# Even and odd heads of an attention layer put into the lower and the upper 64 rows of TensorE's array

## The chip, the cores and the metric

The kernel runs on one core of one Trainium2 chip. The metric is the device time of one execution in microseconds, the median of several. The profiled execution is one more, and every duration below comes from it. PE is TensorE (its weight loads are listed as PEld), DVE VectorE, ACT ScalarE, POOL GpSimdE, SP SyncE, which here only issues DMAs.

## What is computed

The input x holds 64 images of 12 channels and 224 x 224 pixels.

```python
h = einsum("bcij,ce->bije", sums of 16x16 patches, channel_weights)   # 64 x 196 tokens x 192
h = h + single_head_attention(layernorm(h), Wq, bq, Wk, bk, Wv, bv)
h = h + experts(layernorm(h))     # 4 nested experts, each takes its best 98 of the 196 tokens
# inside experts, per image:
q, k, v = qkv.reshape(B, N, 3, 12, 16)...          # 12 heads of 16 columns
attn = softmax(einsum("bhqd,bhkd->bhqk", q, k) * 16 ** -0.5)
x_attn = einsum("bhqk,bhkd->bhqd", attn, v)        # beside gelu(x_mlp), then the second layer (w2)
```

## The kernel before, in words

**Tiling.** Images go in groups of eight (GRP), eight groups in all. A prologue pools and routes the first group; then a loop body runs the attention and the second layer of one group while the next one is pooled (DVE, `pool`), normed and routed (`choose` picks the best tokens). The last group has no next one. Before each group's body stands an opening of eight slots with the hidden layer of its images and the peaks of its first image.

**Order of work.** `body` and `opening` (lines 243 to 347) write out one list of operations: one slot per head, 12 per image, and every engine walks the same list and does its share of each operation. In slot h of image i stand `peak` of image i+1, head h; `score` of image i, head h; then the fill (second layer `fc2` of image i-1, `shift`, `norm_turn`, `project`, `values`, `residual`) and, in slots 1, 5 and 9, the `mix` of four heads. SP walks the list too: the write of the projection (line 709), the stacks (722), the shift row (730) and the output (737).

**Precision by parts.** Query and key are split into a high and a low f16 part (ACT casts at 1192, DVE subtracts at 1445) and written to a scratch in DRAM (709). `stack` reads them back with six DMAs per image into `qs` and `ks`: 16 rows each of (high, high, low) against (high, low, high), so that one matmul over these rows adds the three products. The stacks hold 97 rows: 48 with data, 48 that a memset has zeroed once (1489, 1565), and row 96 for the shift (all ones in `ks`, line 1567).

**Peaks and scores.** For each head PE does two matmuls over 96 rows (`peak`, line 986) into one of two peak banks, head h into bank h % 2, and DVE reduces the bank to the negated maximum of each query (1456). After six heads PE turns the peaks (995), ACT casts them into `shiftT` and one SP DMA puts them into row 96 of `qs` (730). Then two matmuls over 97 rows (`score`, 1005) give the transposed scores less their maximum in one of two score banks, ACT takes the exponential into `Pb` (1205), and `mix` (1020) multiplies with the values: eight matmuls of 32 columns, four heads side by side in four column strips of the array. A matmul in f32 appears in the trace as two.

**Waits.** `peak` waits for its own bank (`peak_free[s]`, counted by DVE), at h = 0 also for the image's stack; `score` waits for its own bank (`score_free[s]`, by ACT), at h = 0 and 6 also for the shift row.

Of the kernel before, what the change touches and what calls it, by code (L numbers as in the profile page):

```python
# [35 lines left out]
T = GRID * GRID  # L36
# [21 lines left out]
KS = 96  # L58
# [350 lines left out]
def bass_vit_tower(nc, x, cw, Wq, bq, Wk, bk, Wv, bv, w_router, gamma, beta, w1, b1, w2, b2, consts, out):  # L409
# [9 lines left out]
    with ctx:  # L419
# [50 lines left out]
        qk16 = sb("qk16", [DC, 2, 2, 2, T], F16)  # L470
        qs = sb("qs", [KS + 1, NSTACK, H, T], F16)
        ks = sb("ks", [KS + 1, NSTACK, H, T], F16)
# [73 lines left out]
        gp_in = sem("gp_in")  # L546
# [123 lines left out]
        def _(sp):  # L670
# [33 lines left out]
            def project(at, G_, dg, i):  # L704

                n_ = G_ * GRP + i
                sp.wait_ge(hi_ready, 2 * n_ + 2)
                sp.wait_ge(lo_ready, 2 * n_ + 2)
                sp.dma_start(qk_dram[i % 2].rearrange("m s c d (h t) -> (d h) (m s c) t", t=T),
                             qk16[:, :, :, :, :].rearrange("p m s c t -> p (m s c) t")).then_inc(qk_out, 16)  # L710

            def stack(at, G_, dg, i):
# [33 lines left out]
        def _(pe):  # L746
# [232 lines left out]
            def peak(at, G_, dg, i, h):  # L979

                s = h % 2
                if h == 0:
                    pe.wait_ge(stack_in[i % NSTACK], 96 * (len(range(i % NSTACK, GRP, NSTACK)) * G_ + i // NSTACK + 1))
# [14 lines left out]
            def score(at, G_, dg, i, h):  # L998

                s = h % 2  # L1000
                if h % 6 == 0:
                    pe.wait_ge(shift_in[h // 6], 16 * (GRP * G_ + i + 1) + ONE)
                pe.wait_ge(score_free[s], 6 * (GRP * G_ + i) + h // 2 + ONE)
                for k in range(2):
                    mm = pe.matmul(score_ps[s][0:HT, T * k:T * k + T],  # L1005
                                   ks[:, i % NSTACK, h, HT * k:HT * k + HT], qs[:, i % NSTACK, h, :],
                                   start=True, stop=True)
                mm.then_inc(score_full[s], 1)
# [57 lines left out]
        def _(act):  # L1066
# [15 lines left out]
            def fuse(at, G_, dg, part):  # L1082
# [8 lines left out]
                for n4, (f, end) in enumerate(M_PARTS):  # L1091
                    dst, src = M[:, f:end], banks[n4][0:U, 0:end - f]
                    if f == HID:
                        dst = dst.rearrange("u (n d h) -> u n h d", d=DH, h=H // 2)
                        src = src.rearrange("u (n h d) -> u n h d", d=DH, h=H // 2)
# [90 lines left out]
            def project(at, G_, dg, i):  # L1186
                n_ = GRP * G_ + i
                act.wait_ge(qk_out, 16 * n_ + ONE)
                for m in range(2):
                    slot, k = at.uses(("qk"[m], (dg, i)))  # L1190
                    act.wait_ge(misc_full[slot], k + 1)
                    act.copy(qk16[:, m, 0, :, :].rearrange("p c t -> p (c t)"), misc_ps[slot][0:DC, 0:2 * T]) \  # L1192
                        .then_inc(hi_ready, 1)

            def shift(at, G_, dg, i, part):
                n_ = GRP * G_ + i
                ps, free = ring(at, "shift", (dg, i, part))
                act.wait_ge(shift_in[part], 16 * n_ + ONE)
                evac(shiftT[:, part, :], ps[0:6, 0:T], free, shift_ready, 2 * n_ + part + 1)

            def score(at, G_, dg, i, h):
                s = h % 2
                n_ = GRP * G_ + i
                act.wait_ge(score_full[s], 6 * n_ + h // 2 + 1)
                act.activation(Pb[:, (H * i + h) % NP, :, :].rearrange("p a b -> p (a b)"), score_ps[s][0:HT, 0:2 * T],  # L1205
# [436 lines left out]
```

## Time and profile before

| | us |
|---|---|
| median of 3 runs | 1775.73 (1774.58 to 1777.63) |
| profiled execution | 1772.98 |
| its span, first to last instruction | 1771.2 |
| PE busy | 1519.9 (86%) |
| DVE busy | 1218.1 (69%) |
| ACT busy | 848.6 (48%) |
| mean granted TensorE clock | 0.921 of full |

Busy time is the union of an engine's instructions over the span. Matmuls overlap, so their mean length is more than the distance between two starts, and the ends of matmuls are modelled. The chain that ended last follows the work back from the last instruction, at each step to what released it. The first 205 us are setup and the prologue; after that a group takes about 201 us, and the last one 155.

### The profile page before, as it was taken

To read this page: it belongs to the slowest core of one execution; us is meant where nothing else is said; L and a number is where in the kernel's file an instruction comes from. 1 tells how busy PE (TensorE), PEld (TensorE's weight loads), DVE (VectorE), ACT (ScalarE), POOL (GpSimd) and SP (SyncE) were. 2 spreads that over 40 slices of the span, in tenths; PEclk is the share of its full clock that TensorE was granted. 3 is DMA by queue.
4 is the path that set the end of the run, shared out by engine and by line. 5 is a ranking of instruction groups with operands and counts; after the bars stand their busy time and mean duration, and the time that the engine had idled before them with its cause. 6 is when DMAs were issued, how large, how long until landed. Compare 5 with 4: busy or idle time off the path is not lost.

```text
span 1771.2 us, 34644 instructions
## 1 busy us (share of the span) xinstructions
PE 1519.9 (86%) x12440; PEld 1260.6 (71%) x12440; DVE 1218.1 (69%) x2822; ACT 848.6 (48%) x1935; POOL 249.4 (14%) x318
## 2 busy tenths in 40 slices
PE   1364689998998899989998899999899889989998
PEld 1233567777786777778787777778677778878786
DVE  3847678766887578865887568875787567563552
ACT  0101355545554555545654554545554555546654
POOL 2012002200121002200121002210022002110000
PEclk9757689989999999999999989989998899989999
DMA  9867376706573357606664356615656151102220
GB/s 225 233 166 195 89 179 158 188 15 161 148 187 99 85 148 178 184 16 158 156 168 117 76 145 168 180 40 136 165 149 148 35 145 45 42 19 59 50 53 15
DMA packets 99598, 218.03 MB, mean 123 GB/s; under 512 B 61371, under 2 KB 75877, under 8 KB 88678
## 3 DMA queue, kind: packets, MB, share of 16 engines
q10 hardware_dynamic: 11904, 149.33, 31.3%
q1 hardware_dynamic: 87526, 66.49, 16.5%
q8 instruction: 102, 1.67, 0.4%
q14 instruction: 66, 0.54, 0.1%
HBM read 186.57 MB, written 28.90 MB: 122 GB/s over the span
## 4 chain that ended last, share of the span: by engine, by line
PE 50%; DVE 25%; issue 13%; DMA 5%; POOL 3%; ACT 2%; SPq 1%; DVEq 0%; ACTq 0%; POOLq 0%
PE bank L1051 13%; DVE psums L1256 10%; DVE peaks L1456 6%; PE bank L956 6%; PE bank L986 5%; PE bank L1020 5%; PE bank L1005 4%; DMA qs<-shiftT 3%; POOL var L1585 3%; PE bank L968 2%; PE bank L879 2%; PE bank L830 2%; PE bank L1029 2%; PE bank L943 2%; DVE qk L1445 1%
## 5 line engine op out<-in xcount | busy, mean ns | idle before, releaser
L1456 DVE TENSOR_REDUCE peaks<-bank 98x2 f32<-98x392 f32 x768 | 423.6, 563 | 170.3 <-PE bank L986 149.3
L1205 ACT ACTIVATE Pb<-bank 98x392 f32<-98x392 f32 x768 | 374.9, 497 | 300.1 <-PE bank L1005 250.9
L1256 DVE TENSOR_REDUCE psums<-xt 112x2 f32<-112x512 f32 x672 | 425.7, 677 | 27.1 <-DVE peaks L1456 9.7
L1051 PE MATMUL bank<-w2T,hid 128*98 128x192 f32 x1536 | 311.4, 342 | 0.0
L986 PE MATMUL bank<-ks,qs 96*98 96x196 f16 x1536 | 268.4, 261 | 42.8 <-DVE peaks L1456 37.9
L1005 PE MATMUL bank<-qs,ks 97*98 97x196 f16 x1536 | 268.3, 258 | 22.1 <-DMA qs<-shiftT 20.2
L986 PEld LDWEIGHTS bank<-ks,qs 96*98 96x98 f16 x1536 | 165.5, 128 | 132.7 <-DVE peaks L1456 66.2
L1051 PEld LDWEIGHTS bank<-w2T,hid 128*98 128x98 f32 x1536 | 249.5, 176 | 3.5
L1005 PEld LDWEIGHTS bank<-qs,ks 97*98 97x98 f16 x1536 | 167.3, 130 | 34.5 <-DMA qs<-shiftT 22.9
L1020 PE MATMUL bank<-Pb,vals 98*32 98x196 f32 x3072 | 171.9, 342 | 1.2 <-ACT Pb L1205 1.2
L1613 POOL TENSOR_TENSOR fin<-fin,both 98x384 f32<-98x384 f32 x64 | 63.9, 999 | 732.9 <-DVE fin L1481 732.9
L956 PE MATMUL bank<-UT,M 104*128 104x196 f32 x768 | 150.8, 347 | 16.9 <-DVEq L1450 16.9
L956 PEld LDWEIGHTS bank<-UT,M 104*128 104x128 f32 x768 | 133.7, 200 | 21.8 <-DVEq L1450 19.3
L1183 ACT ACTIVATE hid<-bank 128x392 f32<-128x392 f32 x192 | 93.5, 497 | 109.9 <-PE bank L956 109.7
L1445 DVE TENSOR_TENSOR qk<-bank,qk 96x392 f16<-96x392 f32 x128 | 71.7, 560 | 84.6 <-ACT qk L1192 74.6
L1576 POOL TENSOR_TENSOR spread_p<-psums,cst 112x196 f32<-112x196 f32 x96 | 50.0, 521 | 533.2 <-DVE psums L1256 533.2
L1020 PEld LDWEIGHTS bank<-Pb,vals 98*32 98x32 f32 x3072 | 81.3, 110 | 54.2 <-issue 25.0
L1117 ACT COPY oT<-bank 128x196 f32<-128x196 f32 x192 | 61.9, 322 | 106.8 <-PE bank L1020 102.4
L1051 PE MATMUL bank<-w2T,onT 96*98 96x192 f32 (+1 forms) x512 | 108.3, 334 | 0.0
L968 PE MATMUL bank<-UT,M 104*96 104x196 f32 x512 | 99.0, 337 | 0.1
L830 PE MATMUL bank<-spread_p,cst 112*24 112x196 f32 x192 | 44.4, 376 | 48.8 <-POOL spread_p L1576 43.3
L1585 POOL TENSOR_TENSOR var<-var,cst 98x16 f32<-98x16 f32 x24 | 69.7, 2904 | 106.7 <-DVE var L1289 58.7
(183 smaller groups left out, 1783.6 us busy)
## 6 DMA issues: line engine op xcount, KB each, us to landing
xt<-in_x_dram ACTq DMA_DIRECT2D x93, 1568.0 KB, 9.0
qk_scratch<-qk SPq DMA_DIRECT2D x64, 294.0 KB, 4.1
qs<-qk_scratch SPq DMA_DIRECT2D x192, 73.5 KB, 3.0
ks<-qk_scratch SPq DMA_DIRECT2D x192, 73.5 KB, 3.1
out_dram<-fin SPq DMA_DIRECT2D x64, 147.0 KB
xt<-in_x_dram SPq DMA_DIRECT2D x3, 1568.0 KB, 8.8
qs<-shiftT SPq DMA_DIRECT2D x128, 2.3 KB
hid<-in_L_ffn_w_dram SPq DMA_DIRECT2D x1, 1440.0 KB
```

The source lines that it names most:

```text
L956: mm = pe.matmul(ps[:, T * j:T * j + T], M[:, 128 * f:128 * f + 128], UT[:, i, :], start=True, stop=True)
L968: mm = pe.matmul(ps[0:DC, T * c:T * c + T], M[:, f:f + DC], UT[:, i, :], start=True, stop=True)
L986: mm = pe.matmul(peak_ps[s][0:HT, T * q:T * q + T], qs[0:KS, i % NSTACK, h, HT * q:HT * q + HT], ks[0:KS, i % NSTACK, h, :], start=True, s ...
L1005: mm = pe.matmul(score_ps[s][0:HT, T * k:T * k + T], ks[:, i % NSTACK, h, HT * k:HT * k + HT], qs[:, i % NSTACK, h, :], start=True, stop=True)
L1020: mm = pe.matmul(ps[32 * j:32 * j + 32, 0:T], vals[:, i % 2, q, h, :], Pb[:, (H * i + h) % NP, q, :], start=(q == 0), stop=(q == 1))
L1051: mm = pe.matmul(misc_ps[slot][0:HT, D * h:D * h + D], lhs, w2T[0:w, f, :], start=(f == 0), stop=(f == NF + 1))
L1183: act.activation(hid[:, i, 2 * b:2 * b + 2, :].rearrange("p a b -> p (a b)"), ps[:, 0:2 * T], ACT.Gelu).then_inc(free, 1)
L1205: act.activation(Pb[:, (H * i + h) % NP, :, :].rearrange("p a b -> p (a b)"), score_ps[s][0:HT, 0:2 * T], ACT.Exp, scale=float(DH) ** -0.5 ...
L1256: last = dve.tensor_reduce(psums[:, m % 2, t, 2 * p:2 * p + 2], v[:, 2 * p:2 * p + 2, :, :], AX.XY, ALU.add)
L1445: dve.tensor_tensor(qk16[:, m, 1, :, :].rearrange("p c t -> p (c t)"), misc_ps[slot][0:DC, 0:2 * T], qk16[:, m, 0, :, :].rearrange("p c t ...
L1456: dve.tensor_reduce(peaks[:, h // 6, :, h % 6], peak_ps[s][0:HT, 0:2 * T].rearrange("p (q k) -> p q k", q=2), AX.X, ALU.max, negate=True). ...
L1585: gp.tensor_tensor(var[:, 2, :], var[:, 1, :], const("half", HT), ALU.pow).then_inc(gp_pow, 1)
```

## The change

Even heads lie in rows 0 to 63 of the stacks and odd heads in rows 64 to 127, each with 48 rows of data and the shift in the 49th. The zero rows go. Peaks and scores are issued for two heads at a time, in even slots: first columns of the even and of the odd head, then the second columns of both. Each half has its own bank. Both banks are waited for ahead of the first matmul. The fill of the slots keeps its order. The columns of the projection are laid out anew (when M is copied, with one ACT copy more), so that heads of one parity lie together; ACT and DVE write the high and low parts to other places of `qk16`. The stack of an image is read with eight DMAs in place of six (the same bytes), and each shift part with two in place of one. The memset of `qs` goes and those of `ks` become smaller.

```diff
-KS = 96
+KS = 3 * DH
+ODD = 64
...
-        qs = sb("qs", [KS + 1, NSTACK, H, T], F16)
-        ks = sb("ks", [KS + 1, NSTACK, H, T], F16)
+        qs = sb("qs", [2 * ODD, NSTACK, H // 2, T], F16)
+        ks = sb("ks", [2 * ODD, NSTACK, H // 2, T], F16)
...
             def stack(at, G_, dg, i):
...
-                for blk, (qp, kp) in enumerate(((0, 0), (0, 1), (1, 0))):
-                    for m, st, part in ((0, qs, qp), (1, ks, kp)):
-                        sp.dma_start(st[DH * blk:DH * blk + DH, s, :, :].rearrange("d (c h) t -> d c (h t)", c=2),
-                                     qk_dram[i % 2, m, part].rearrange("c d w -> d c w")) \
+                for m, st in enumerate((qs, ks)):
+                    for c in range(2):
+                        both_ = qk_dram[i % 2, c, m].rearrange("s d w -> (s d) w")
+                        low = ODD * c
+                        sp.dma_start(st[low:low + 2 * DH, s, :, :].rearrange("d h t -> d (h t)"), both_) \
                             .then_inc(stack_in[s], 16)
+                        sp.dma_start(st[low + 2 * DH:low + KS, s, :, :].rearrange("d h t -> d (h t)"),
+                                     both_[DH * (1 - m):DH * (1 - m) + DH, :]).then_inc(stack_in[s], 16)
...
-                sp.dma_start(qs[KS:KS + 1, i % NSTACK, 6 * part:6 * part + 6, :],
-                             shiftT[:, part, :]).then_inc(shift_in[part], 16)
+                for c in range(2):
+                    sp.dma_start(qs[ODD * c + KS:ODD * c + KS + 1, i % NSTACK, 3 * part:3 * part + 3, :],
+                                 shiftT[3 * c:3 * c + 3, part, :]).then_inc(shift_in[part], 16)
...
             def peak(at, G_, dg, i, h):
-                s = h % 2
+                if h % 2:
+                    return
...
-                pe.wait_ge(peak_free[s], 6 * (GRP * G_ + i) + h // 2 + ONE)
+                for s in range(2):
+                    pe.wait_ge(peak_free[s], 6 * (GRP * G_ + i) + h // 2 + ONE)
                 for q in range(2):
-                    mm = pe.matmul(peak_ps[s][0:HT, T * q:T * q + T],
-                                   qs[0:KS, i % NSTACK, h, HT * q:HT * q + HT], ks[0:KS, i % NSTACK, h, :],
-                                   start=True, stop=True)
-                mm.then_inc(peak_full[s], 1)
+                    for s in range(2):
+                        mm = pe.matmul(peak_ps[s][0:HT, T * q:T * q + T],
+                                       qs[ODD * s:ODD * s + KS, i % NSTACK, h // 2, HT * q:HT * q + HT],
+                                       ks[ODD * s:ODD * s + KS, i % NSTACK, h // 2, :], start=True, stop=True)
+                        if q == 1:
+                            mm.then_inc(peak_full[s], 1)
...
             def score(at, G_, dg, i, h):
...
+                for s in range(2):
+                    pe.wait_ge(score_free[s], 6 * (GRP * G_ + i) + h // 2 + ONE)
                 for k in range(2):
+                    for s in range(2):
+                        mm = pe.matmul(score_ps[s][0:HT, T * k:T * k + T],
+                                       ks[ODD * s:ODD * s + KS + 1, i % NSTACK, h // 2, HT * k:HT * k + HT],
+                                       qs[ODD * s:ODD * s + KS + 1, i % NSTACK, h // 2, :], start=True, stop=True)
+                        if k == 1:
+                            mm.then_inc(score_full[s], 1)
...
-            dve.memset(qs[:, :, :, :], 0.0)
...
-            gp.memset(ks[:, :, :, :], 0.0).then_inc(gp_in, 1)
-            gp.wait_ge(gp_in, 1)
-            gp.memset(ks[KS:KS + 1, :, :, :], 1.0).then_inc(zeroed, 1)
+            gp.memset(ks[ODD // 2:ODD, :, :, :], 1.0)
+            gp.memset(ks[ODD + ODD // 2:2 * ODD, :, :, :], 1.0).then_inc(zeroed, 1)
```

DVE's `peak` and ACT's `score` change likewise: in even slots they reduce, or exponentiate, first the even and then the odd head. The peaks of the even heads of a part come first in `peaks`, then those of the odd heads.

## Rows read from the trace of the kernel before

**Rows 1.** The page: span, busy time and share of two engines, the chain by engine.
```profile
span 1771.2 us, 34644 instructions
...
PE 1519.9 (86%) x12440; PEld 1260.6 (71%) x12440; DVE 1218.1 (69%) x2822; ACT 848.6 (48%) x1935; POOL 249.4 (14%) x318
...
PE 50%; DVE 25%; issue 13%; DMA 5%; POOL 3%; ACT 2%; SPq 1%; DVEq 0%; ACTq 0%; POOLq 0%
```

**Rows 2.** Busy time by stretch: from:to, us, each engine, then clock, DMA share, GB/s.
```profile
674.00:704.00 30.00, 28.89 (x253) 24.30 (x251) 26.29 (x56) 14.28 (x34) 8.33 (x12) 1.00 0.57 142
704.00:730.00 26.00, 25.86 (x231) 21.77 (x230) 20.73 (x45) 16.29 (x38) 5.41 (x11) 1.00 0.71 183
...
1600.00:1760.00 160.00, 150.77 (x1376) 128.81 (x1375) 76.26 (x167) 94.36 (x212) 8.43 (x9) 0.99 0.19 45
```

The engines in this view stand in the order PE, PEld, DVE, ACT, POOL.

**Rows 3.** The chain in order of time, 640 to 842 us: start, length, what.
```profile
654.20 6.28 DMA qs<-shiftT
...
751.75 1.92 PE bank L1051 x6
...
775.83 0.98 PE bank L1051 x6
```

**Rows 4.** Groups of instructions: busy us, mean ns | idle before, and who ended it.
```profile
L1456 DVE TENSOR_REDUCE peaks<-bank 98x2 f32<-98x392 f32 x768 | 423.6, 563 | 170.3 <-PE bank L986 149.3 <-DVE on_tok L1469 1.1 <-DVE qk L1445 0.8
...
L986 PE MATMUL bank<-ks,qs 96*98 96x196 f16 x1536 | 268.4, 261 | 42.8 <-DVE peaks L1456 37.9 <-DMA ks<-qk_scratch 0.2
L1005 PE MATMUL bank<-qs,ks 97*98 97x196 f16 x1536 | 268.3, 258 | 22.1 <-DMA qs<-shiftT 20.2 <-ACT Pb L1205 1.6
```

**Rows 5.** Timeline of PE from 778.4 us; one row of its weight loads last.
```profile
778.48 0.81 PE L1051 MATMUL bank<-w2T,onT 96*98 96x192 f32 x4
779.22 0.87 PE L1020 MATMUL bank<-Pb,vals 98*32 98x196 f32 x16
780.02 0.37 PE L986 MATMUL bank<-ks,qs 96*98 96x196 f16 x2
780.23 0.33 PE L1005 MATMUL bank<-qs,ks 97*98 97x196 f16 x2
780.40 0.33 PE L986 MATMUL bank<-ks,qs 96*98 96x196 f16 x2
780.57 0.33 PE L1005 MATMUL bank<-qs,ks 97*98 97x196 f16 x2
...
780.32 0.21 PEld L986 LDWEIGHTS bank<-ks,qs 96*98 96x98 f16 x2
```

**Rows 6.** Timeline of PE in the setup, transposes of line 814.
```profile
59.80 0.26 PE L814 MATMUL bank<-cst,hid 64*96 64x64 f32 x1
59.99 0.31 PE L814 MATMUL bank<-cst,hid 128*96 128x128 f32 x1
60.14 0.93 PE L814 MATMUL bank<-cst,hid 128*96 128x128 f32 x7
```

**Rows 7.** Who waited for whom: us in total, times, longest us.
```profile
PE bank L986 <- DVE peaks L1456: 37.9, 65, 1.4
...
PE bank L1005 <- DMA qs<-shiftT: 20.2, 13, 3.6
```

**Rows 8.** SP's queue: its longest wait, and its issues (ns min/median/max).
```profile
SPq L730 <- ACT shiftT L1117: 680.6, 128, 11.6
...
L730 SPq DMA_DIRECT2D qs<-shiftT x128: 664/685/741, 223.0 to 1746.0; - x128
...
L722 SPq DMA_DIRECT2D ks<-qk_scratch x192: 414/424/2179, 202.3 to 1720.5; - x192
```

**Rows 9.** Busy time around a stretch at half clock (columns as in rows 2).
```profile
745.60:749.00 3.40, 1.32 (x9) 0.78 (x10) 2.07 (x9) 0.71 (x4) 1.93 (x2) 1.00 1.04 270
749.00:755.80 6.80, 6.80 (x31) 5.90 (x30) 4.65 (x13) 1.67 (x4) 2.90 (x1) 0.50 0.78 169
```

More of the change, by code:

```diff
@@ L998, in score @@
             def score(at, G_, dg, i, h):
-                s = h % 2
+                if h % 2:
+                    return
                 if h % 6 == 0:
-                    pe.wait_ge(shift_in[h // 6], 16 * (GRP * G_ + i + 1) + ONE)
-                pe.wait_ge(score_free[s], 6 * (GRP * G_ + i) + h // 2 + ONE)
+                    pe.wait_ge(shift_in[h // 6], 32 * (GRP * G_ + i + 1) + ONE)
+                for s in range(2):
+                    pe.wait_ge(score_free[s], 6 * (GRP * G_ + i) + h // 2 + ONE)
                 for k in range(2):
[L1005 to L1008, printed above, removed]
+                    for s in range(2):
[4 more added lines that the diff above has]
+                            mm.then_inc(score_full[s], 1)
             def mix(at, G_, dg, i, c):
@@ L1093, in fuse @@
                     if f == HID:
-                        dst = dst.rearrange("u (n d h) -> u n h d", d=DH, h=H // 2)
-                        src = src.rearrange("u (n h d) -> u n h d", d=DH, h=H // 2)
+                        dst = dst.rearrange("u (m c d h) -> u m c d h", m=2, c=2, d=DH)
+                        src = src.rearrange("u (m h c d) -> u m c d h", m=2, c=2, d=DH)
+                        act.copy(dst[:, 0], src[:, 0])
+                        dst, src = dst[:, 1], src[:, 1]
                     last = act.copy(dst, src)
@@ L1191, in project @@
                     act.wait_ge(misc_full[slot], k + 1)
-                    act.copy(qk16[:, m, 0, :, :].rearrange("p c t -> p (c t)"), misc_ps[slot][0:DC, 0:2 * T]) \
+                    act.copy(qk16[:, :, 1 + m, :], misc_ps[slot][0:DC, 0:2 * T].rearrange("p (c t) -> p c t", c=2)) \
                         .then_inc(hi_ready, 1)
@@ L1197, in shift @@
                 ps, free = ring(at, "shift", (dg, i, part))
-                act.wait_ge(shift_in[part], 16 * n_ + ONE)
+                act.wait_ge(shift_in[part], 32 * n_ + ONE)
                 evac(shiftT[:, part, :], ps[0:6, 0:T], free, shift_ready, 2 * n_ + part + 1)
             def score(at, G_, dg, i, h):
-                s = h % 2
+                if h % 2:
+                    return
                 n_ = GRP * G_ + i
-                act.wait_ge(score_full[s], 6 * n_ + h // 2 + 1)
-                act.activation(Pb[:, (H * i + h) % NP, :, :].rearrange("p a b -> p (a b)"), score_ps[s][0:HT, 0:2 * T],
-                               ACT.Exp, scale=float(DH) ** -0.5).then_inc(score_free[s], 1)
+                for s in range(2):
+                    act.wait_ge(score_full[s], 6 * n_ + h // 2 + 1)
+                    act.activation(Pb[:, (H * i + h + s) % NP, :, :].rearrange("p a b -> p (a b)"),
+                                   score_ps[s][0:HT, 0:2 * T],
+                                   ACT.Exp, scale=float(DH) ** -0.5).then_inc(score_free[s], 1)
             def mix(at, G_, dg, i, c):
@@ L1444, in project @@
                     dve.wait_ge(hi_ready, n_)
-                    dve.tensor_tensor(qk16[:, m, 1, :, :].rearrange("p c t -> p (c t)"),
-                                      misc_ps[slot][0:DC, 0:2 * T],
-                                      qk16[:, m, 0, :, :].rearrange("p c t -> p (c t)"),
+                    dve.tensor_tensor(qk16[:, :, 3 * m, :],
+                                      misc_ps[slot][0:DC, 0:2 * T].rearrange("p (c t) -> p c t", c=2),
+                                      qk16[:, :, 1 + m, :],
                                       ALU.subtract).then_inc(lo_ready, 1)
@@ L1452, in peak @@
             def peak(at, G_, dg, i, h):
-                s = h % 2
+                if h % 2:
+                    return
                 n_ = 6 * (GRP * G_ + i) + h // 2 + 1
-                dve.wait_ge(peak_full[s], n_)
-                dve.tensor_reduce(peaks[:, h // 6, :, h % 6],
-                                  peak_ps[s][0:HT, 0:2 * T].rearrange("p (q k) -> p q k", q=2),
-                                  AX.X, ALU.max, negate=True).then_inc(peak_free[s], 1)
-                if h % 6 == 5:
-                    dve.wait_ge(peak_free[s], n_ + ONE)
+                for s in range(2):
+                    dve.wait_ge(peak_full[s], n_)
+                    dve.tensor_reduce(peaks[:, h // 6, :, h % 6 // 2 + 3 * s],
+                                      peak_ps[s][0:HT, 0:2 * T].rearrange("p (q k) -> p q k", q=2),
+                                      AX.X, ALU.max, negate=True).then_inc(peak_free[s], 1)
+                if h % 6 == 4:
+                    for s in range(2):
+                        dve.wait_ge(peak_free[s], n_ + ONE)
                     dve.sem_inc(peaks_ready, 1)
```

9 lines of the change are left out of this document (4 added, 5 removed).

## The prediction

> **What bounds the kernel now.** I read the page first [rows 1]: PE is busy for 86% of the span, DVE for 69%, and the chain that ended last is half PE and a quarter DVE. An average over stages says little, so I then read one group of eight images, from 640 to 842 us, by stages and beside it the chain in order of time [rows 2, 3]. The reader is to see that the stages differ. From 674 to 704 us DVE is busy for 26.3 of 30 us and the chain hops from one DVE instruction to the next (sums of the next group, peaks, first-layer maxima). From 704 to 730, 747 to 760 and 770 to 813 us it runs over PE (fc2, hidden, mixes). Adding up the chain's PE stretches (641 to 644, 660 to 674, 704 to 730, 747 to 760, 770 to 813, 817 to 828 and 834 to 838 us) gives 113 of the 202 us. One matmul cut out of PE is therefore worth its price in a little over half of a full group. In the last group no new images are pooled, DVE is busy for 76 of 160 us, PE for 151, and PE's time counts almost in full (last line of [rows 2]).
>
> **What a head costs now.** Peaks and scores are 1536 matmuls each [rows 4], two per head. Their means (261 and 258 ns) are lengths from issue to result; what they cost is the distance from one start to the next. In a stretch without waits the starts lie at 780.23, 780.40 and 780.57 us, so one head of peaks or of scores costs 0.17 us [rows 5]. Their weight load costs nothing there, because it starts one matmul ahead: at 780.32 for the matmul of 780.40.
>
> **The array's halves.** With 48 or 49 rows at row 0 and at row 64 an even and an odd head can stream together. No row of this trace shows two row halves at once; the bounds are 0.17 us for two heads (full overlap) and 0.34 (none). The nearest row is the mix: 16 matmuls into four column strips take 0.80 us from 779.22 to 780.02, four waves at 0.165 with four matmuls in each and one change of form [rows 5], while one f32 matmul of fc2 costs 0.163 alone (0.98 for six) [rows 3]. Four strips at once cost what one does, so I take full overlap, 0.175 us for two heads. That saves 0.165 us per pair. A full group has 48 pairs of peaks and 48 of scores: 96 x 0.165 = 15.8 us.
>
> **What it pays for that.** The trace charges for each change between forms of the array. From fc2 (four matmuls, 0.65) at 778.48 to the mix at 779.22 are 0.74 us, 0.09 more; after a mix the same 0.09 comes again, and the next weight load lies bare: the head at 780.02 is 0.21 long, not 0.17 [rows 5]. Forms cut by rows pay too: a 64-row transpose in the setup starts at 59.80 us and its 128-row neighbour at 59.99, 0.19 later, though it streams half as many columns as the 128-row ones, which lie 0.11 apart (seven of them from 60.14, 0.93 to the end of the last, 0.27 long) [rows 6]. The Trainium skill says the same against this change ("TensorEngine Tiling (Array Packing)", Key Properties): changing the tiling mode, not just the tile, drains TensorE. It gives no price; by the rows it is 0.09. I counted the changes of form along PE's order, written out by the planner. Peaks and scores of a pair mostly stand together and are followed by full-height work or a mix. A full group goes from 66 changes to 141: 75 x 0.09 = 6.8 us. Loads laid bare: 32 entries from full-height work at 0.04 = 1.3; 47 exits, of which 31 into f32 matmuls, whose 98 to 128 columns of weights have about 0.08 to lose, and 16 into transposes or the like at 0.04: 3.1. Net for PE in a full group: -15.8 + 6.8 + 1.3 + 3.1 = -4.6 us. Added up operation by operation, half of it falls into the PE stretches named above, because the pairs alone in the opening (peaks without scores, +0.13 each) stand there too: -2.3. Seven such groups: -16.1. The last group: 90 pairs save 14.9, 58 more changes cost 5.2, bare loads 3.3: -6.4. The prologue's six lone pairs: +0.8. **Sum on PE: -21.7 us.**
>
> **Waits.** A pair now waits for both peak banks and both score banks. Behind that wait on PE's queue stand the scores, fc2 and everything else; DVE and ACT wait for these. Today PE waits 37.9 us, 65 times, for DVE's peaks [rows 7]. At worst each of those waits grows by the odd head's reduction, 0.563 us [rows 4]: +36. At best they vanish, -38: DVE now gets both reductions ahead of the other work of two slots, ahead of the projection's two subtractions above all. DVE waits for PE's peaks four times as long (149.3 us [rows 4]) as PE for it, and after both reductions it has 1 to 2 us of other work before it needs the next pair, against the 0.2 us of PE's reply. I take 0. ACT is busy for little more than half of any stretch in [rows 2]: 0.
>
> **SyncE's queue.** The shift row is sent by two DMAs in place of one, 128 more issues at 0.685 us [rows 8]. They are behind a wait for ACT's shiftT, and both must land before the first score of a half. PE waits for this DMA 13 times, 20.2 us in all [rows 7]. If the second issue delays each: 13 x 0.685 = +8.9; if the landing is set by what else the DMA engines move (one chain piece has 6.28 us from issue to use, nine times the issue [rows 3]), 0. I take half, +4.5. The stacks are eight DMAs per image where there were six, the same bytes: 128 more issues at 0.42 = 54 us of SyncE's time. The queue waits 680.6 us for shiftT alone [rows 8], and a stack is due one image later: 0. If that cover went, PE's wait for the stack (0.2 us today, under ks<-qk_scratch in [rows 4]) would grow first. The projection's write keeps its size.
>
> **Clock.** In this group PE runs at half its rate (1.2 in place of 2.4 GHz) four times. In the 3.4 us ahead of the first of them it had been busy for 1.32 us, and then for all of 6.8 us at half rate [rows 9]. At half rate six matmuls of fc2 take 1.92 in place of 0.98 us [rows 3]. The halves make PE stream less, and in stretches where DVE or a DMA sets the pace nothing fills the hole. Bounds: no further stretch, 0; one of 6.8 us in each of eight groups, half of it lost, +27. I take one of 3.4 us in every second full group, 1.7 lost in each, and as much again in longer ones: +6.
>
> **Setup.** The memset of qs goes and those of ks shrink; they run before the first tile of x is there, which DVE waits for. The copy of M gets one instruction more, once: 0. Subtractions and casts of q and k keep their shapes: 0.
>
> **Sum.** -21.7 + 4.5 + 6 = -11.2. The profiled execution took 1773.0 us (its span 1771.2 [rows 1]), 2.7 under the median of 1775.7. 1773.0 - 11.2 = 1761.8, and with those 2.7 the median forecast is **1764.5 us**.
>
> **Rivals.**
> First, **no overlap** (the change doesn't do what it says): the two halves stream one after the other. Then the 0.165 are not saved and the changes of form are paid: +11.2 us on PE per full group, half of it in the chain, 7 x 5.6, last group +8.5, prologue +1.8, with shift and clock +10.5: 1836 us. For it: no row shows two row halves together. Against: the column strips, in the same rows as above. It decides if over 0.29 us of the 0.34 remain. 10%.
> Second, **partial overlap**: both halves' weights come one after the other, and each wave lays one load bare, 0.04. 192 waves: +7.7 us, so +3.1 per full group, 7 x 1.55, last group +0.8, prologue +1.3, others +10.5: 1799 us. For it: a bare load shows as 0.04 at each entry. Against: the mix, where four matmuls and their four loads fit into one wave. 12%.
> Beside this stands the Trainium skill ("TensorE: Matmul & The Clock Gate", Measured speedup vs the span model): four row strips ran 3.07 times as fast, 0.77 of full; no run here shows it. By that figure a pair would cost 0.22 us and the time would be about 1785, an estimate from that page.
> Third, **the clock**, the case that ends on the other side: PE drops to half rate in one 6.8 us stretch more per group, +27 in place of +6: 1785 us; it decides from about 2 us lost per group. For it: the stretches where PE waits for a shift or for POOL are at the edge already. Against: where PE sets the pace it is busy throughout, 25.9 of 26 us [rows 2]. 12%.
> Fourth, **both banks as one** on DVE's side: the +36 above, 1800 us. For it: the DVE stretch from 674 to 704 us. Against: the order of work on DVE. 8%.
>
> **Chances and range.** My forecast 53%, with its own range 1738 (two thirds of the peak waits vanish, -26) to 1772 (the whole 8.9 for the shift row, and 3 more for the clock). The four rivals 42%; the rest is a change too small to see. About 0.2%, 3.6 us, is what a measurement can tell from no change. Faster 0.53; same 0.12, from the forecast's upper end and the weak forms of the third and fourth case; slower 0.35. The range 1738 to 1801 leaves out the first rival and the tails.
>
> **What the new profile would show.** Right: in a stretch without waits, even and odd head start within some 10 ns, the next pair's start lies 0.17 to 0.18 us behind; PE's matmuls of peaks and scores have about half the busy time of today's 268 us each; idle put down to "issue" before them grows by 51 x 0.25 us or so per group; the reductions of DVE come in twos. Wrong: starts of the halves 0.08 us apart (first rival), pairs at 0.21 or more (second), more than five half-rate stretches per group (third), PE's wait for DVE's peaks above 60 us (fourth), PE's wait for the shift row above 30 us.

## The result, and the profile after

The changed kernel took 1812.6 us (median of 4 runs, 1810.3 to 1815.5) against 1776.7 for the kernel before (1774.6 to 1781.0): a ratio of 1.020, interval 1.018 to 1.023. That is 36 us slower, where 11 us faster had been forecast, and above the upper end of the range (1801). Ratios leave out executions more than 1.5% above the fastest of the same kernel, so they need not be the quotient of the medians.

The page of the kernel after: span, busy time of the engines, granted clock in 40 slices, and the chain by engine, as in [rows 1].

```profile
span 1813.7 us, 35428 instructions
...
PE 1521.1 (84%) x12440; PEld 1167.1 (64%) x12440; DVE 1208.7 (67%) x2821; ACT 809.4 (45%) x1936; POOL 242.7 (13%) x318
...
PEclk9757789888997879979798879979888899989898
...
PE 49%; DVE 24%; issue 12%; DMA 6%; POOL 3%; SPq 3%; ACT 2%; DVEq 0%; POOLq 0%; ACTq 0%
```

PE is busy for 1521 us, as long as before (1520), though its two f16 groups have lost nearly half their time: other work of PE has become longer (L1063 below was 311.4 us before). The next views show where. First the groups of instructions, as in [rows 4]: busy us, mean ns | idle before.

```profile
L1063 PE MATMUL bank<-w2T,hid 128*98 128x192 f32 x1536 | 323.1, 356 | 0.0
L993 PE MATMUL bank<-ks,qs 48*98 48x196 f16 x1536 | 154.4, 281 | 80.9 <-DVE peaks L1475 71.9 <-DMA ks<-qk_scratch 8.5
...
L1016 PE MATMUL bank<-qs,ks 49*98 49x196 f16 x1536 | 148.0, 272 | 20.5 <-DMA qs<-shiftT 14.5 <-ACT Pb L1221 5.9
```

Peaks and scores (L993, L1016) went from 268 us each to 154 and 148. The idle time before the peaks grew from 42.8 to 80.9 us. Then the timeline of PE in a stretch at full clock.

```profile
702.46 0.37 PE L993 MATMUL bank<-ks,qs 48*98 48x196 f16 x4 [0.36 <-DVE peaks L1475]
702.64 0.36 PE L1016 MATMUL bank<-qs,ks 49*98 49x196 f16 x4
702.94 0.33 PE L1003 MATMUL bank<-cst,peaks 98*6 98x98 f32 x2
```

Four matmuls, a pair of heads, take 0.18 us from start to start, where one head took 0.17 [rows 5]: the halves do stream together. After the scores the exit from the 64-row form (the array split into two halves of rows) shows: 0.30 us to the next operation instead of 0.17 or 0.18. Ahead of the pair of peaks PE has waited 0.36 us for DVE. Now who waited for whom (us in total, times, longest).

```profile
PEld bank L993 <- issue: 92.0, 273, 2.2
...
PE bank L993 <- DVE peaks L1475: 71.9, 74, 2.1
...
PE bank L1016 <- DMA qs<-shiftT: 14.5, 11, 2.0
```

The wait for DVE's peaks nearly doubled (37.9 in [rows 7]), the one for the shift row fell (20.2), and the weight loads of peaks sat idle under "issue" for 92.0 us, 50.4 before. Last, the stretches at half clock (1.2 in place of 2.4 GHz); columns as in [rows 2], the clock third from the end.

```profile
762.30:776.00 13.70, 11.62 (x58) 8.09 (x58) 8.48 (x27) 3.32 (x10) 6.29 (x3) 0.50 0.57 154
...
864.70:885.20 20.50, 19.61 (x132) 12.79 (x131) 15.06 (x30) 10.48 (x26) 0.52 (x1) 0.50 0.39 96
```

Before, no half-clock stretch between 250 and 1350 us was longer than 6.8 us. Adding up the granted clock's record from 205 us on gives 347 us at half clock in 41 stretches, against 167 in 32 before. A group in the middle has five or six such stretches, 48 to 58 us together; before it had four or five, 20 to 24 us.

So four things stand in the profile: overlap (gain), changes of form, a longer wait for a bank, and more half-clock time. The experiments price the first three; the clock moves with each of them and isn't separated.

### The profile page after: what moved, and what is told of

Its sections match the earlier page's. It is cut to its first block, busy times and chain, and to the rows that moved or that the text cites. A ratio compares the mean times of both kernels' runs of the same rounds, so it can differ in the third digit from the quotient of the medians.

```text
span 1813.7 us, 35428 instructions
## 1 busy us (share of the span) xinstructions
PE 1521.1 (84%) x12440; PEld 1167.1 (64%) x12440; DVE 1208.7 (67%) x2821; ACT 809.4 (45%) x1936; POOL 242.7 (13%) x318
## 4 chain that ended last, share of the span: by engine, by line
PE 49%; DVE 24%; issue 12%; DMA 6%; POOL 3%; SPq 3%; ACT 2%; DVEq 0%; POOLq 0%; ACTq 0%
PE bank L1063 13%; DVE psums L1273 9%; DVE peaks L1475 7%; PE bank L960 6%; PE bank L1032 5%; PE bank L993 4%; PE bank L972 3%; DMA ks<-qk_scratch 3%; POOL var L1603 3%; PE bank L1016 3%; PE bank L883 2%; PE bank L1041 2%; PE bank L834 2%; PE bank L947 2%; DVE nm L1320 1%
## 5 line engine op out<-in xcount | busy, mean ns | idle before, releaser
L1475 DVE TENSOR_REDUCE peaks<-bank 98x2 f32<-98x392 f32 x768 | 398.1, 561 | 183.4 <-PE bank L993 171.0
L1221 ACT ACTIVATE Pb<-bank 98x392 f32<-98x392 f32 x768 | 339.3, 494 | 255.2 <-PE bank L1016 233.9
L1063 PE MATMUL bank<-w2T,hid 128*98 128x192 f32 x1536 | 323.1, 356 | 0.0
L1063 PEld LDWEIGHTS bank<-w2T,hid 128*98 128x98 f32 x1536 | 265.1, 182 | 16.9 <-issue 5.8
L993 PE MATMUL bank<-ks,qs 48*98 48x196 f16 x1536 | 154.4, 281 | 80.9 <-DVE peaks L1475 71.9
L993 PEld LDWEIGHTS bank<-ks,qs 48*98 48x98 f16 x1536 | 71.0, 128 | 189.6 <-issue 92.0
L1032 PE MATMUL bank<-Pb,vals 98*32 98x196 f32 x3072 | 186.0, 364 | 1.4 <-ACT Pb L1221 1.4
L1016 PE MATMUL bank<-qs,ks 49*98 49x196 f16 x1536 | 148.0, 272 | 20.5 <-DMA qs<-shiftT 14.5
L1462 DVE TENSOR_TENSOR qk<-bank,qk 96x392 f16<-96x392 f32 x128 | 71.9, 561 | 93.7 <-ACT qk L1206 82.9
L1016 PEld LDWEIGHTS bank<-qs,ks 49*98 49x98 f16 x1536 | 91.2, 137 | 35.4 <-DMA qs<-shiftT 17.0
L1063 PE MATMUL bank<-w2T,onT 96*98 96x192 f32 (+1 forms) x512 | 112.9, 344 | 0.0
L972 PEld LDWEIGHTS bank<-UT,M 104*96 104x96 f32 x512 | 83.4, 173 | 13.1 <-issue 3.8
```

What stands on the lines that cost most here:

```text
L972: mm = pe.matmul(ps[0:DC, T * c:T * c + T], M[:, f:f + DC], UT[:, i, :], start=True, stop=True)
L993: mm = pe.matmul(peak_ps[s][0:HT, T * q:T * q + T], qs[ODD * s:ODD * s + KS, i % NSTACK, h // 2, HT * q:HT * q + HT], ks[ODD * s:ODD * s + ...
L1016: mm = pe.matmul(score_ps[s][0:HT, T * k:T * k + T], ks[ODD * s:ODD * s + KS + 1, i % NSTACK, h // 2, HT * k:HT * k + HT], qs[ODD * s:ODD ...
L1032: mm = pe.matmul(ps[32 * j:32 * j + 32, 0:T], vals[:, i % 2, q, h, :], Pb[:, (H * i + h) % NP, q, :], start=(q == 0), stop=(q == 1))
L1063: mm = pe.matmul(misc_ps[slot][0:HT, D * h:D * h + D], lhs, w2T[0:w, f, :], start=(f == 0), stop=(f == NF + 1))
L1221: act.activation(Pb[:, (H * i + h + s) % NP, :, :].rearrange("p a b -> p (a b)"), score_ps[s][0:HT, 0:2 * T], ACT.Exp, scale=float(DH) ** ...
```

## The experiments

Beside each set of runs the kernel before ran on the same chip (medians of 1774.6 to 1777.4 us, from 12 to 19 runs); ratios are to it. Half-clock times and waits are those of one profiled execution.

**1. Pairs in full height** (e1): the kernel before with heads issued in pairs and both banks waited for, on the old 96-row stacks.

```diff
+                if h % 2:
+                    return
+                for s in range(2):
+                    pe.wait_ge(peak_free[s], 6 * (GRP * G_ + i) + h // 2 + ONE)
+                for s in range(2):
+                    for q in range(2):
...
```

> The kernel before with peaks, scores, reductions and exponentials in pairs and both banks waited for, but each head still over 96 or 97 rows: nothing overlaps, no form of the array changes, the DMAs stay. Theory 'clock' (the change loses its time because PE streams fewer columns and so runs longer at half clock): PE streams as much as before, so the half-clock time after 205 us stays within 30 us of before's 167 us and the time within 0.5% of 1776 (1768 to 1786). Theory 'both banks' (the joint wait is what costs): most of the 36 us of the change is here, 1800 to 1815, with PE's wait for DVE's peaks above 60 us.

1797.2 us, ratio 1.014 (1.010 to 1.018), clock 0.912. More than half of the loss comes without any half of the array. PE's wait for DVE's peaks was 69.7 us and half clock 200 us.

**2. Everything twice in the halves** (e2): the kernel after with each matmul of peaks and scores repeated (`for q in (0, 0, 1, 1)`).

> The changed kernel with each matmul of peaks and scores done twice, so that PE streams for them as long as before the change (0.35 us for a pair in place of 0.175), with all the changes of form besides: PE has some 16 us more to do per group. Theory 'clock': the half-clock time falls from 347 us towards 170 to 220, and the extra work costs little or nothing: 1795 to 1820 us, no slower than the change. Theory 'changes of form' or 'both banks' (the clock is a result, not the cause): the extra streaming comes on top, 8 to 16 us per group, 1875 to 1930 us.

1850.0 us (1.041; 1.037 to 1.045), 37 above the kernel after by the medians, for some 130 us more of streaming on PE, between the two expectations. Half clock was 174 us in place of 347, in the fastest of the four runs (granted clock 0.921, 0.910 in the others, 0.872 in the kernel after). So 127 us of streaming are worth 37 us here, under a third: a first hint that what the overlap saves is worth less than forecast.

**3. The DMAs alone** (e3): the kernel before with eight stack DMAs per image and two for each shift row.

```diff
+                for c in range(2):
+                    sp.dma_start(qs[KS:KS + 1, i % NSTACK, 6 * part + 3 * c:6 * part + 3 * c + 3, :],
+                                 shiftT[3 * c:3 * c + 3, part, :]).then_inc(shift_in[part], 16)
```

> The kernel before with the change's DMAs alone: eight for each stack and two for each part of the shift row. My sum had +4.5 us for this, bounds 0 and 9. Theory 'clock' and theory 'both banks': 1776 to 1786. Theory 'DMAs' (SP's longer queue delays the shift row and the stacks): at least half of the 36 us, 1795 or more, with PE's wait for the shift row above 35 us in place of 20.

1774.4 us, ratio 0.9985 (0.996 to 1.001); PE waits 15.2 us for the shift row, 13 times, and 4.2 us for the stack (0.2 before). The DMAs cost nothing that can be measured.

**4 and 5. PE kept busy** (e4 on the kernel after, e5 on the kernel before): extra f32 matmuls into banks about to be overwritten, at four places where PE is short of work.

```diff
+            def busy(bank, n):
+                for _ in range(n):
+                    pe.matmul(bank[:, 0:T], ident, cst[:, 0:T], start=True, stop=True)
...
+                busy(ps, 7)
```

> The changed kernel with useless f32 matmuls (0.165 us for each of the two parts of one) into the bank about to be written, ahead of PE's long waits: 3 at planes, 7 at chosen, 6 at the first hidden of a group, 2 at each pair of peaks of the second image. They add work but no result. Theory 'clock': half-clock time after 205 us falls from 347 us below 200 and the time falls by 10 to 45 us, to 1765 to 1800. Theories 'both banks' and 'changes of form': no gain, 1812 to 1830.

1813.7 us (1.0225; 1.020 to 1.025), half clock 160 us in place of 347, clock 0.931: the clock came back and the time stayed. The extra work took 122 us of PE's busy time, so this run alone doesn't say what the clock was worth.

> The kernel before with the same extra f32 matmuls as e4 (three at each image pair's planes, seven ahead of the choice, six ahead of the first hidden, one per peak of image 1), which raised the clock of the kernel after from 0.872 to 0.931 and left its time at 1813.7. Theory A (the extra matmuls themselves cost PE time, and in the kernel after the clock's return paid for them): the kernel before, whose clock was 0.921, has little to get back and pays, 1785 to 1800. Theory B (the extra matmuls lie in idle time and cost nothing, so the clock was worth nothing either): 1770 to 1780.

1810.7 us (1.020; 1.013 to 1.027), half clock 68 us. That is more than the 1785 to 1800 of the nearer expectation. The same extra work costs the kernel before 34 us and the kernel after 1. I read the difference as the clock: of the kernel after 187 us of half clock were taken away, of the kernel before 100, and the 87 us between them paid 32 us, 0.37 us each. This isn't shown: it supposes that the extra work alone costs both the same, and with the joint wait PE waits 83.5 us for DVE's peaks in e4 (58.3, and 25.2 ahead of the extra matmuls), 32.7 in e5.

**6. Pairs, each head with its own wait** (e6): e1, with the wait for a bank directly ahead of that head's matmuls.

```diff
                 for s in range(2):
                     pe.wait_ge(peak_free[s], 6 * (GRP * G_ + i) + h // 2 + ONE)
-                for s in range(2):
                     for q in range(2):
```

> e1 (the kernel before, full height, heads issued in pairs) came out at 1797.2 us. Here PE waits for a head's own bank just before that head's two matmuls instead of for both banks ahead of the pair; VectorE and ScalarE still take two heads in a row. Theory A, the joint wait costs the time (the pair starts only when the later of two banks is free): back to about 1778, within 5. Theory B, the order costs it (a pair of peak reductions or exponentials placed in one slot delays what stood between them): it stays at 1797, within 5.

1771.8 us, ratio 0.9987 (0.9955 to 1.002): no loss. The waits of PE's peaks in e1:

```profile
PE bank L989 <- DVE peaks L1467: 69.7, 80, 1.7
...
PE bank L989 <- DMA ks<-qk_scratch: 11.1, 7, 2.7
```

and in e6:

```profile
PE bank L988 <- DVE peaks L1465: 31.7, 44, 1.3
...
PE bank L988 <- DMA ks<-qk_scratch: 13.0, 7, 2.6
```

The order on VectorE and ScalarE is the same in both, and the late stack is alike (11 and 13 us), half clock nearly so (200 and 184 us). Of PE's waits the one for VectorE differs most, 38 us; the one for ScalarE's exponentials is 3.8 us in e1 and 0.8 in e6. The joint waits, for peak and score banks together, cost 25 us, nothing else in the pairs does. How they do is my reading: two banks become one, PE stands while DVE reduces the second head, then DVE stands while PE streams (DVE's wait for PE's peaks is 154.9 us in e1, 142.6 in e6).

**7 and 8. Only peaks, only scores in pairs** (e7, e8): the parts of e1.

> The kernel before with only the peaks in pairs (PE with both banks waited for, VectorE two reductions in a row); scores as before. Theory A, what VectorE gives back late is what PE waits for (in e1 the wait of the peak matmuls on VectorE's peaks was 69.7 us against 37.9): nearly all of e1's 21 us, 1790 to 1797. Theory B, it is the scores, whose pair puts two exponentials in front of ScalarE's other evacuations and shifts the project step and its stack transfer: under 5 us, 1775 to 1781.

> The kernel before with only the scores in pairs. Theory A of e7: 1775 to 1781. Theory B of e7: 1790 to 1797. If the two parts add, this run and e7 together lose e1's 21 us.

1795.7 and 1795.8 us (both 1.012; 1.007 to 1.017 and 1.006 to 1.018). Each part alone loses nearly all of what both lose. They don't add, and neither theory fitted. In e7 PE waits 63.9 us for VectorE's peaks. Why scores alone lose as much isn't settled, since PE's wait there for VectorE's peaks is 42.7 us and for ScalarE 10.1: the wait for the peaks isn't the whole of what a joint wait costs. Scores in pairs with own waits alone were not run.

**9. Halves, one head per slot** (e9): the kernel after with the old slots, own waits, no pairs.

> The kernel after with its 64-row halves and stacks, but one head per slot with its own bank's wait, as before: no two halves meet except where one head's last matmul stands beside the next head's first. Theory A, the pairing and its waits cost 21 us and the halves themselves cost only their change of form: PE streams as much as before plus up to 7 us of changes per group hidden in part, 1776 to 1795. Theory B, the halves are what costs (changes of form and clock): no better than the kernel after, 1808 to 1830, since the overlap is lost as well.

1968.1 us, ratio 1.110 (1.103 to 1.116), far outside both theories. From 205 us on PE enters or leaves the 64-row form 1402 times instead of 816. Half clock was 454 us, in an execution in which PE was busy for 89% of the span, more than in any other. The 27.3 us from 691 us on are one stretch at half clock, columns as above:

```profile
691.00:718.30 27.30, 26.53 (x144) 17.06 (x144) 17.22 (x34) 12.13 (x28) 0.52 (x1) 0.50 0.38 90
```

**10 and 11. Halves with own waits.** e10 waits for the odd bank after the first even matmul; e11 issues even 0, even 1, wait, odd 0, odd 1; its edit, made alike in `score`:

```diff
                 for s in range(2):
                     pe.wait_ge(peak_free[s], 6 * (GRP * G_ + i) + h // 2 + ONE)
-                for q in range(2):
-                    for s in range(2):
+                    for q in range(2):
```

> The kernel after, but PE waits for the second bank only after the first matmul of the even head: even 0, wait, odd 0, even 1, odd 1; still two heads at a time. In full height the pair with a joint wait cost 21 us (1797.2) and the pair with each head's own wait nothing (1771.8). Theory A, it is the joint wait in the kernel after too, and one matmul ahead of it is enough: 1790 to 1800. Theory B, the halves' interleaved order hands both banks over together at the end of the pair, so that VectorE and ScalarE still start late and the next pair still waits for the second of two reductions: 1806 to 1815, little better than the kernel after (1812.6).

> The kernel after in the order even 0, even 1, wait, odd 0, odd 1: each head's bank is handed over as early as in the full-height pairs with own waits, one entry and one exit of the 64-row form per pair as in the kernel after, but only one of the two halves streams at a time save where even 1 meets odd 0. Theory A (early hand-over is worth more than the overlap): 1785 to 1800. Theory B (the changes of form cost on their own: one head at a time they cost 193 us over 768 visits, 0.25 us each; in pairs there are half as many visits, some 96 us, no longer paid by the overlap of 0.165 us per two matmuls): 1830 to 1880.

1803.7 us (1.016; 1.008 to 1.024) and 1804.6 (1.017; 1.010 to 1.024). Both lie between their two expectations. All eight runs (1796 to 1808) lie below all four of the kernel after (1810 to 1816), though the intervals of the ratios overlap. The wait for VectorE's peaks fell to 44.4 and 40.2 us. e11 should have lost its overlap by my own reckoning, but it did not. Its timeline, with the odd bank free at 703.8 and late at 710.0:

```profile
703.81 0.37 PE L992 MATMUL bank<-ks,qs 48*98 48x196 f16 x4
704.02 0.34 PE L1014 MATMUL bank<-qs,ks 49*98 49x196 f16 x4
704.28 1.57 PE L972 MATMUL bank<-UT,M 104*96 104x196 f32 x8
...
710.05 0.70 PE L992 MATMUL bank<-ks,qs 48*98 48x196 f16 x3
710.47 0.28 PE L1014 MATMUL bank<-qs,ks 49*98 49x196 f16 x1
```

Four matmuls again pass in 0.21 us. The single records show even 0 at 703.812, odd 0 at 703.819, even 1 at 703.935, odd 1 at 703.941; which record is which follows from the semaphores recorded with them (the odd bank's wait stands at the second record, the even bank's increment at the third). So by the records the odd head overtook the even head's second matmul. That happened in 304 of 384 pairs of peaks and 301 of 384 of scores. Where the odd bank is late, both even matmuls go first. The Trainium skill ("TensorE: Matmul & The Clock Gate", The mechanism) has matmuls in strict order of issue; the records of e11 don't agree.

**12. Extra matmuls ahead of the choice alone** (e13): the kernel before plus the seven of e5 in each group, where PE waits for VectorE's choice.

> The kernel before with only the seven extra matmuls ahead of the choice. There PE stands idle while VectorE chooses; in e4 the stretch from the peaks of image 6 on was 3.5 us per group shorter than in the kernel after. Theory A (half clock in the opening of a group costs, and work in the idle stretch ahead of it returns it): 1745 to 1768. Theory B (VectorE sets the end of that stretch whatever the clock): 1772 to 1782.

1753.1 us (10 runs, 1746.0 to 1762.0), ratio 0.988 (0.985 to 0.991): the one version that beats both kernels. Half clock fell from 167 to 105 us. From the first reduction of one group to that of the next, four groups in the middle took 196.5, 199.8, 196.2 and 202.4 us, before 201.4, 201.2, 203.8 and 205.2.

**13 and 14. The same seven on pairs** (e14 on e6, e15 on e10).

> Full-height pairs with own waits (e6, 1771.8) plus the seven extra matmuls ahead of the choice, which took the kernel before from 1777.1 to 1753.1. If pairs with own waits are worth nothing and the filler's gain is its own, 1746 to 1756; if fewer visits of PE per head help once the clock is up, below 1745; if the two hinder each other (e6 had the image stack landing late seven times), 1757 to 1770.

> The halves with the second bank waited for after the first matmul (e10, 1803.7, half clock 327 us) plus the same seven extra matmuls. Theory A (the clock is what the halves lose): the filler returns more here than the 24 us of the kernel before, 1755 to 1772. Theory B (changes of form are what they lose): it returns 24 us or less, 1780 to 1795, and stays some 30 us behind e14.

1773.2 us (0.998; 0.994 to 1.002) and 1797.6 (1.014; 1.008 to 1.020). Both lie above their expectations, and the gain isn't carried over: half clock stays at 181 us in e14 (184 in e6) and at 304 in e15 (327 in e10). Why the order of the pairs keeps its half-clock stretches wasn't tried.

**15 to 17. Changes of form alone** (e16, again as e19 in more rounds) and their control (e17): e6 with one small matmul ahead of each pair of peaks, over 48 rows (64-row form) or over 96.

```diff
+                    if s == 0:
+                        pe.matmul(peak_ps[0][0:HT, 0:8], qs[0:48, i % NSTACK, h, 0:HT],
+                                  ks[0:48, i % NSTACK, h, 0:8], start=True, stop=True)
```

> Full-height pairs with own waits (e6) plus one matmul of 48 rows and 8 columns in the 64-row form ahead of each pair of peaks: PE enters and leaves the 64-row form 384 times more, and streams 3072 columns more in all, about 1.3 us. Theory A (changes of form cost what they show, 0.09 us and more each, part of it on the path): 25 to 60 us above e6, 1797 to 1832, and above e17. Theory B (they hide in PE's idle time, the halves lose by the clock): within 8 us of e17.

> The control for e16: the same small matmul with 96 rows, in the form of the pair itself. Both theories: within 8 us of e6, 1766 to 1780, since it only adds a weight load of 98 columns and 8 streamed columns per pair.

> The same kernel as e16, whose runs took 1790 to 1829 us. If its fast runs again stand 20 to 45 us above e17's 1778.0, the changes of form are shown; below 1785 they were not what e16 paid.

e16: 1819.4 us (four runs, 1790 to 1829; 1.017; 1.005 to 1.029). e19: 1822.8 (1811 to 1827), ratio 1.024 (1.021 to 1.027). e17: 1778.0, ratio 1.002 (0.999 to 1.005). The timeline of e19:

```profile
700.70 0.20 PE L988 MATMUL bank<-ks,qs 48*98 48x8 f16 x1
700.84 0.54 PE L991 MATMUL bank<-ks,qs 96*98 96x196 f16 x4
```

and of e17:

```profile
703.19 0.17 PE L988 MATMUL bank<-ks,qs 96*98 96x8 f16 x1
703.22 0.52 PE L991 MATMUL bank<-ks,qs 96*98 96x196 f16 x4
```

From the small matmul to the pair are 0.14 us with a change of form and 0.03 without (up to 0.07 elsewhere in e17), so that a change shows as 0.07 to 0.11 us, around the 0.09 of [rows 5]. The weight loads' idle time under "issue" goes the way of the kernel after, in e19:

```profile
PEld bank L988 <- issue: 82.5, 282, 1.1
PE bank L988 <- DVE peaks L1468: 20.0, 39, 1.3
```

against 42.4 us, 114 times, in e17. PE's busy time is 1607.8 us in e19 and 1542.1 in e17, 0.086 us more for each of the 768 changes. In time they cost 45 us by the medians (1822.8 - 1778.0) and 39 by the ratios, 51 to 58 ns each, nearly two thirds of the 0.09 us that one shows on PE. Half clock is 225 us, 194 in e17, so a part of this comes by way of the clock.

**18. Half the columns** (e18): e6 with 98 streamed columns in place of 196 in five pairs of six; about 105 us less to stream (3072 matmuls x 5/6 x 98 columns at 2.4 GHz). The kernel leaves out the other half of these products, and its exponential has a scale near zero, so only its time counts.

> Full-height pairs with own waits (e6, 1771.8) that stream 98 columns instead of 196 in the peaks and scores of five pairs of each six, about as much less as the overlap saves, with no 64-row form. It leaves out the other half of those products, and the exponential's scale is near zero. Theory A (the saved columns lie on PE's path, and the halves lose by changes of form): 1735 to 1755. Theory B (fewer columns lengthen the half-clock time, which takes them back): half clock well above e6's 184 us and a time of 1762 to 1780.

1766.4 us (9 runs, 1746.9 to 1780.4), ratio 0.991 (0.987 to 0.994). Against e6 that is 5 us by the medians, 14 by the ratios. Page and waits of e18's profiled execution (its fastest):

```profile
span 1745.1 us, 34596 instructions
...
PE 1459.2 (84%) x12440; PEld 1202.6 (69%) x12440; DVE 1207.7 (69%) x2822; ACT 804.7 (46%) x1935; POOL 248.7 (14%) x318
```

```profile
PE bank L988 <- DVE peaks L1467: 49.8, 111, 1.7
...
PE bank L1010 <- DMA qs<-shiftT: 17.1, 12, 4.9
```

Peaks and scores are busy for 335 us, in e6 for 435: 100 less. All of PE has only 65 less (1524.0 in e6), so by this account the other matmuls took 35 us more; half clock rose from 184 to 252 us. And PE waits longer for VectorE's peaks (49.8, in e6 31.7) and for the shift row (17.1 and 9.0). Theory A fell and theory B came, in its time and in its sign. By the forecast's price of 0.56 the 105 us were worth 59. An estimate accounts for most of what is missing: 68 us more of half clock at the 0.37 of e4 and e5 are 25 us, and PE's waits for peaks, shift row and stack are 23 us longer. So the saved columns seem to go into clock and waits; how much into which isn't shown.

## Why the prediction was wrong

The parts, put together from the runs and beside my terms:

| term | forecast | measured, from |
|---|---|---|
| pairs as such | 0 | -3, e6 to the kernel before beside it; not clear of zero |
| less streaming | -71 | -7 to -17, e18 scaled from 105 to 127 us; -37, e2 |
| changes of form, loads laid bare | +50 | +34 to +47, e19 to e17, scaled |
| joint wait | 0 | +6 to +8, kernel after to e11 (+25 in full height) |
| DMAs of the shift row | +4.5 | 0, e3 |
| clock, as a term | +6 | not separated; lies in the terms above |
| sum | -11 | +20 to +45 by e18, 0 to +15 by e2; the result was +36 |

The forecast's second and third entry are my -21.7 taken apart: 11.2 us of changes and loads per full group, half of them in the chain for seven groups, 8.5 in the last and 1.8 in the prologue make 50, and the rest is streaming. The changes are scaled in two ways: entries and exits of the 64-row form from 768 to 816 (+42 to +47), or changes of any form, of which e19 has 609 more than e17 and the kernel after 520 more than before, since many of its exits go straight into a mix (+34 to +38). The result lies inside the sum by e18 and above that by e2, so the parts explain the direction and most of the size, not every microsecond.

- **Overlap**: right. Full overlap and 0.175 us per pair were forecast; the trace shows 0.18, the two heads' starts lie under 10 ns apart in 383 of 384 pairs of peaks and 318 of 384 of scores. The rivals "no overlap" and "partial overlap" fell, and with the second the 0.22 us worked out beside it: the Trainium skill ("TensorE: Matmul & The Clock Gate", Measured speedup vs the span model) has four row strips at 0.77 of full, and two halves here lose nothing that the timeline shows. The groups' busy time halved, as forecast (154 and 148 of 268 us).
- **Changes of form**: right in size (+50 forecast, +34 to +47 measured). The rule of the Trainium skill ("TensorEngine Tiling (Array Packing)", Key Properties) that a change of mode drains TensorE names no cost; the runs don't show the drain itself, but a cost of each change: 0.09 us on PE and 51 to 58 ns of time. But I had forecast 51 x 0.25 us per group of "issue" before the f16 matmuls, and before the peaks it grew by 42 us in all, before the scores by 10 (13.4, 3.2 before).
- **The step that failed** is the first one: "One matmul cut out of PE is therefore worth its price in a little over half of a full group." The chain told me what bound the end of this execution, not what happens when work is taken away from those stretches. By it the overlap was to bring 71 us of the 127 that it saves. 105 us less to stream were worth 5 to 14 us (e18), and 127 more in the halves 37 (e2): scaled, 7 to 37 us. The 0.56 of the chain (114 of 202 us; the 113 is a slip of no weight) is not a price. What is added there costs (e19: 39 to 45 us for 66 on PE), what is taken away mostly isn't gained, as e18 shows, where the waits for DVE and the shift row and the half-clock time grew.
- **The clock** was a term of its own in my sum, with the sign right and the size far off: +180 us of half-clock time in place of some 30. What it is worth stays open. By the 0.37 us of e4 and e5 (e13 gives 0.39, 24 us for 62) the 180 would be some 67 us, an estimate that rests on what was supposed there; e14 and e15, where the same matmuls returned nothing, show that it is no fixed price. It can't be added to the ledger, since e18 and e19 already hold a part of it, and that the clock carries more of the loss than the form changes isn't excluded. The third rival (one longer stretch per group) came in kind and went well beyond its 6.8 us. I had looked for "more than five half-rate stretches per group"; there are five or six, only longer.
- **Both banks as one**, my fourth rival, had 8%; its mechanism took part, though the time didn't come from it alone. Its mark, PE's wait for DVE's peaks above 60 us, came at 71.9. I argued against it from the order of work on DVE and took the middle of -38 and +36. e1 against e6 measures +25 in full height. In the halves it costs 6 to 8. Why less isn't shown; my guess is that PE is late there by the changes of form anyway.
- **DMAs**: the half of 8.9 was too much, e3 shows nothing; the stacks' zero was right in time. The wait for the stack did grow as the forecast had feared, from 0.2 to 8.5 us, but it was 13.0 us in e6, without the extra DMAs and without a loss.

Still open: why the pair of scores alone loses as much as the pair of peaks (e7, e8), how the 193 us of e9 split between changes and clock, and how much of the kernel's own 36 us is the clock.

## What to carry to other kernels

Packing two small matmuls into the array's halves is likely to pay only where they stand together for long: here a visit to the 64-row form held about two pairs (768 in 408 visits) at 0.165 us saved, and paid 0.09 on the way in and again on the way out. On PE's account that was a small gain; in time the changes counted for over half of their length and the saving for about a tenth (e18) or at most three tenths (e2). When two units of work are issued together, let each wait for its own buffer; a wait for both cost 25 us in full height. And before believing in work taken off the busiest engine, stream less of it in an experiment: this one, 105 us less for 5 to 14 us, would have put the forecast in doubt at once.

## What the runs showed of the hardware

- By the trace's records TensorE ran two halves' matmuls out of their order of issue (304 of 384 pairs of peaks in e11), and the overlap was the same for both orders of issue.
- A change between the 64-row form and full height showed as about 0.09 us on PE and cost 51 to 58 ns of time (e19 against e17).
- Half clock was 454 us in the execution with PE's highest busy share (89%, e9), so the busy share alone did not tell the clock.
- With 105 us less to stream, half clock rose from 184 to 252 us (e6 to e18).
- Seven matmuls whose results are thrown away, per group of images, in a stretch where PE waits, made the kernel before 24 us faster (e13). The same seven did nothing measurable for pairs (e14).
